# Two quarters to a step in a fused linear-attention and LoRA mixture kernel on one Trainium2 core

## What is computed

```python
def attention(q, k, v):            # EMB_DIM here is the 512 rows, 8 heads of 64
    qh = softmax(qh, axis=3)       # over the rows of a head
    kh = softmax(kh, axis=1)       # over the columns, the kernel's other axis
    kvs = einsum('bnhd,bnhe->bhde', kh, vh)
    return einsum('bnhd,bhde->bnhe', qh, kvs)

def lora_moe(x, router_w, A, B):   # 4 experts, the best 2 are used, rank 16
    logits = flat @ router_w.T
    gates = softmax(top-2 of logits, -inf elsewhere)
    mid = einsum('tf,erf->ter', flat, A)
    all_deltas = einsum('ter,eor->teo', mid, B) * 4
    return einsum('te,teo->to', gates, all_deltas)

x = x + attention(layernorm(x), ctx, ctx)
x = x + lora_moe(layernorm(x), router_w, A, B)
```

## Time and profile before

| | |
|---|---|
| median of three runs | 456.83 us |
| profiled execution | 454.94 us |
| its span | 453.2 us |
| TensorE busy, matmuls / weight loads | 422.5 us (93%) / 382.3 us (84%) |
| VectorE busy | 379.1 us (84%) |
| GpSimd busy | 358.9 us (79%) |
| ScalarE busy | 311.0 us (69%) |
| mean granted TensorE clock | 0.969 of full |
| moved | 137.59 MB, 304 GB/s on average |
| chain that ended last | TensorE 71%, VectorE 10%, GpSimd 6% |

### The profile page before, as it was taken

How to read it: one execution, slowest core, us unless ns; L and a number is a source line. 1 busy time by engine, 2 the same in 40 slices (tenths; PEclk the granted TensorE clock), 3 DMA queues, 4 the chain that set the end, 5 groups by cost and what they waited for, 6 DMA issues and landing times.

```text
span 453.2 us, 16801 instructions
## 1 busy us (share of the span) xinstructions
PE 422.5 (93%) x6888; PEld 382.3 (84%) x6888; DVE 379.1 (84%) x1045; ACT 311.0 (69%) x436; POOL 358.9 (79%) x343
## 2 busy tenths in 40 slices
PE   6558998999999999999999999999999999999975
PEld 6557887898989898998989898998989898999864
DVE  3468777898998989898998989898989989775864
ACT  1265979695968778695958777785959777775310
POOL 0466999999898989898898989898988988994610
PEclk9667999999999999999999999999999999999988
DMA  8995888779999999999999999999999998454247
GB/s 286 420 409 188 307 290 271 248 276 321 364 297 372 339 340 344 307 341 332 351 310 361 331 346 341 307 352 333 357 316 338 310 366 269 173 186 187 95 185 279
DMA packets 38972, 137.59 MB, mean 304 GB/s; under 512 B 4208, under 2 KB 6384, under 8 KB 38768
## 3 DMA queue, kind: packets, MB, share of 16 engines
q1 hardware_dynamic: 38896, 136.52, 86.5%
HBM read 102.95 MB, written 33.55 MB: 301 GB/s over the span
## 4 chain that ended last, share of the span: by engine, by line
PE 71%; DVE 10%; POOL 6%; DMA 4%; issue 3%; SPq 3%; ACT 1%; POOLq 0%; DVEq 0%; ACTq 0%
PE num_ps L407 21%; PE kv_ps L390 14%; PE raw_ps L423 11%; PE delta_ps L471 10%; PE kv_ps L438 6%; PE delta_ps L472 6%; DMA ctx_sb<-in_ctxt_dram 4%; DVE y_sb L709 3%; POOL y_sb L323 3%; POOL ek_sb L311 3%; DVE attnT L700 2%; DVE bn_parts L642 2%; DVE midT L800 1%; PE raw_ps L457 1%; SPq L235 1%
## 5 line engine op out<-in xcount | busy, mean ns | idle before, releaser
L311 POOL TENSOR_TENSOR ek_sb<-ctx_sb,kmax_row 128x512 f32<-128x512 f32 x128 | 167.8, 1313 | 36.5 <-ACT kmax_row L504 36.5
L323 POOL TENSOR_TENSOR y_sb<-attnT,y_sb 128x512 f32<-128x512 f32 x128 | 164.3, 1284 | 31.0 <-DVE attnT L700 31.0
L407 PE MATMUL num_ps<-kv_sb,x_sb 128*128 128x130 f32 x1024 | 141.1, 281 | 9.0 <-DVE attnT L700 6.0
L407 PEld LDWEIGHTS num_ps<-kv_sb,x_sb 128*128 128x128 f32 x1024 | 126.0, 192 | 12.9 <-issue 8.7
L709 DVE TENSOR_TENSOR y_sb<-delta_ps,y_sb 128x512 f32<-128x512 f32 x128 | 87.3, 684 | 23.7 <-PE delta_ps L472 22.8
L625 DVE TENSOR_REDUCE max_n<-ctx_sb 128x32 f32<-128x512 f32 x128 | 86.5, 677 | 10.8 <-DMA ctx_sb<-in_ctxt_dram 10.8
L390 PE MATMUL kv_ps<-ctx_sb,ek_sb 128*64 128x65 f32 x2048 | 92.8, 233 | 0.3 <-ACT ek_sb L526 0.3
L700 DVE TENSOR_TENSOR attnT<-num_ps,rden 128x512 f32<-128x512 f32 x128 | 88.5, 691 | 4.8 <-DVE rden L697 0.4
L390 PEld LDWEIGHTS kv_ps<-ctx_sb,ek_sb 128*64 128x64 f32 x2048 | 74.2, 139 | 17.8 <-issue 5.8
L526 ACT ACTIVATE ek_sb<-ek_sb 128x1024 f32<-128x1024 f32 x64 | 67.1, 1049 | 26.9 <-POOL ek_sb L311 26.9
L423 PE MATMUL raw_ps<-w_sb,y_sb 128*64 128x69 f32 x2048 | 84.5, 223 | 0.0
(11 more groups left out here) (63 smaller groups left out, 398.3 us busy)
## 6 DMA issues: line engine op xcount, KB each, us to landing
ctx_sb<-in_ctxt_dram SPq DMA_DIRECT2D x64, 520.0 KB, 5.3
x_sb<-in_x_dram SPq DMA_DIRECT2D x64, 512.0 KB, 6.1
y_sb<-in_xt_dram SPq DMA_DIRECT2D x64, 512.0 KB, 6.3
out_dram<-y_sb SPq DMA_DIRECT2D x60, 512.0 KB, 6.2
out_dram<-y_sb SPq DMA_DIRECT2D x8, 256.0 KB, 3.6
sq_a<-in_bt_dram SPq DMA_DIRECT2D x1, 1024.0 KB, 15.8
w_sb<-in_wt_dram SPq DMA_DIRECT2D x1, 552.0 KB, 9.6
cst<-in_consts_dram SPq DMA_DIRECT2D x1, 145.0 KB, 2.3
```

What stands on the lines that cost most here:

```text
L311: pool.tensor_tensor(ek_sb[:, t % 2, chunks(g), :].rearrange("p (a b) c -> p a b c", b=2), ctx_sb[:, t % 4, 2 * g:2 * g + 2, 1:P + 1, :].r ...
L323: pool.tensor_tensor(y, attnT[:, g, :], y, ALU.add).then_inc(x1_made, 1)
L407: mm = pe.matmul(num_ps[:, j // 2, at:at + 2 * (DH + 1)], x_sb[:, t % 4, c * P:(c + 1) * P], kv_sb[:, t % 2, :], start=True, stop=True, sk ...
```

## The change

The step becomes two quarters: every engine's loop runs over q in twos, and calls helpers for q and q + 1. FIRST is -10 and LAST is 4 NT + 20. TensorE's calls are put in order by the tile shape they use. The two delta banks become one buffer of two banks, and one `add_delta` takes both. max_ps moves from num_ps to delta_ps. `root1` and `root2` stand between GpSimd's large operations. VectorE's gate and layernorm operations are spread between the large ones, and `normalise` is split into `invert` and `normalise`. The three gate stages stand at offsets 16, 18 and 20, in three consecutive steps. b is loaded after the first ctx, x and y tiles into slot 7 of y_sb, and split in steps 8 to 12. The last stores are four of 512 KB in place of eight of 256 KB.

```diff
-    FIRST = -8
-    LAST = 4 * (NT - 1) + 29
+    FIRST = -10
+    LAST = 4 * NT + 20
...
-        delta_ps = [bank("delta_ps0"), bank("delta_ps1")]
-        max_ps = num_ps[:, 0, 3 * P:4 * P]
+        delta_ps = bank("delta_ps", (P, 2, 512))
+        max_ps = delta_ps[:, 0, 0:P]
...
-            p, i = divmod(q - 21, 8)
+            p, i = divmod(q - 22, 8)
...
             whole(load_ctx, 1)
-            sp.dma_start(w_sb[:], wt).then_inc(w_landed, 16)
             whole(load_x, 1)
             whole(load_ctx, 2)
+            sp.dma_start(w_sb[:], wt).then_inc(w_landed, 16)
             whole(load_y, 0)
-            sp.dma_start(b_rows, bt).then_inc(b_landed, 16)
-            whole(load_y, 1)
             whole(load_x, 2)
             whole(load_ctx, 3)
+            whole(load_y, 1)
+            sp.dma_start(b_rows, bt).then_inc(b_landed, 16)
...
-            for q in range(FIRST, LAST + 1):
-                root1(q)
-                shift(*tile_at(q, -3))
-                root2(q)
-                add_x(*tile_at(q, 5))
+            for q in range(FIRST, LAST + 1, 2):
+                shift(*tile_at(q, -2))
+                add_x(*tile_at(q, 6))
+                root2(pair_in(q, 18))
+                shift(*tile_at(q + 1, -2))
+                root1(tile_in(q, 2))
+                add_x(*tile_at(q + 1, 6))
...
-                after(pe, out_made, 8 * p + i - 1)
+                if i % 2 == 0:
+                    after(pe, out_made, 4 * p + i // 2)
+                    after(pe, kmax_made, min((8 * p + i + 22) // 4 + 2, NT))
...
+            for q in range(FIRST, LAST + 1, 2):
+                turn_max(tile_in(q, -4))
+                numerator(*tile_at(q, 6))
                 delta(*delta_at(q))
-                turn_max(q)
+                delta(*delta_at(q + 1))
+                sum_squares(tile_in(q, 12))
+                turn_mid(pair_in(q, 20))
...
+                spread_kmax(tile_in(q, -4))
+                numerator(*tile_at(q + 1, 6))
+                for k in range(2):
+                    kv(*tile_at(q + k, 0))
+                for k in range(2):
+                    project(*tile_at(q + k, 8))
+                fold_squares(tile_in(q, 10))
...
+            for q in range(FIRST, LAST + 1, 2):
+                T = q // 4
+                if q % 4 == 0:
+                    copy_squares(T - 3)
+                    copy_kv(T - 1)
+                    keys(T, 0)
+                    spread_row(T + 1)
+                    mid_high(pair_in(q, 20))
                     square_x1(T - 2, 0)
+                    queries(T - 1, 0)
                     sum_x(T + 1)
+                else:
                     keys(T, 1)
                     square_x1(T - 2, 1)
+                    gate_exp(pair_in(q, 18))
                     queries(T - 1, 1)
                     square_x(T + 1)
...
             def add_delta(p, i):
-                dve.wait_ge(delta_done, 8 * p + i + 1)
-                y = y_sb[:, pair_slots(p), 2 * i:2 * i + 2, :]
+                dve.wait_ge(delta_done, 8 * p + i + 2)
+                y = y_sb[:, pair_slots(p), 2 * i:2 * i + 4, :]
...
+            for q in range(FIRST, LAST + 1, 2):
+                a, b, c = pair_in(q, 16), pair_in(q, 18), pair_in(q, 20)
+                kv_recip(tile_in(q, 4), 0)
+                if c is not None:
+                    gate_gates(c)
+                kv_recip(tile_in(q, 4), 1)
                 if c is not None:
                     gate_mid(c)
+                max_whole(tile_in(q, -4))
+                invert(*tile_at(q, 6))
+                if b is not None:
+                    gate_rank(b)
+                ln1_bias(tile_in(q, 4))
+                normalise(*tile_at(q, 6))
+                add_delta(*delta_at(q))
+                invert(*tile_at(q + 1, 6))
+                if a is not None:
+                    gate_logits(a)
+                    gate_max(a)
+                if b is not None:
+                    gate_select(b)
+                ln1_mean(tile_in(q, -2))
+                normalise(*tile_at(q + 1, 6))
+                mid_low(c)
+                ln1_aggr(tile_in(q, 0))
                 if a is not None:
                     gate_centre(a)
+                    gate_below(a)
+                    gate_beats(a, 0)
+                    gate_beats(a, 1)
                 if b is not None:
+                    gate_sum(b)
+                    max_part(*tile_at(q, -8))
+                    gate_recip(b)
+                    max_part(*tile_at(q + 1, -8))
+                    gate_scale(b)
+                else:
+                    max_part(*tile_at(q, -8), P // 2)
                 if a is not None:
+                    gate_mask(a)
+                for k in range(2):
+                    bn_part(*tile_at(q + k, -4))
+                ln1_var(tile_in(q, 0))
```

More of the change, by code:

```diff
@@ L791, in gate_mid, with mid_low @@
                         ALU.mult).then_inc(mid_made, 1)
[L793 to L794 removed]
+            def mid_low(p):
                 if p is None:
@@ L801, in mid_low @@
                                   ALU.subtract).then_inc(lo_made, 1)
-            for q in range(FIRST, LAST + 1):
-                early = q < 0
-                if early:
-                    max_whole(q)
-                a, b, c = pair_at(q, 13), pair_at(q, 14), pair_at(q, 15)
-                if b is not None:
-                    gate_beats(b, 0)
+            for q in range(FIRST, LAST + 1, 2):
[4 more added lines that the diff above has]
+                kv_recip(tile_in(q, 4), 1)
@@ L819, in _ @@
-                mid_low(q)
-                bn_part(*tile_at(q, -5))
-                add_delta(*delta_at(q))
-                if a is not None:
-                    gate_logits(a)
-                if b is not None:
-                    gate_rank(b)
-                if not early:
-                    max_whole(q)
-                normalise(*tile_at(q, 5))
-                if a is not None:
-                    gate_below(a)
-                if b is not None:
-                    gate_select(b)
-                    gate_sum(b)
-                    gate_scale(b)
```

196 lines of the change are left out of this document (83 added, 113 removed).

## The result

The changed kernel takes 481.87 us (median of 6 runs, 480.67 to 483.14) against 456.41 us for the kernel before (6 runs): ratio 1.056, 95% interval 1.0539 to 1.0581. Forecast were 467.0 us and a range of 451 to 476. The direction was right, the size lay outside the range. The profiled execution has a span of 479.4 us, 26.2 more than before; forecast were 10.2 more.

The account below looks back on a forecast made before the run. It took TensorE as the bound (24.88 us busy of a 25.24 us pair), VectorE and GpSimd close behind. Start +0.3, steps 22 to 128 +0.2 and end +9.7 sum to +10.2 us: median 467.0 us, range 451 to 476.

Parts of the forecast that it names:

- The start to step 6: Loads of b and second y tile moved back: taken as 5 us, step 6 at 33.3 instead of 38.29.
- The splitting of b: Start, steps 6 to 22: splitting on ScalarE and VectorE now lies here, 1.5 us by estimate.
- The gate's wait in step 18: Start, before step 22: the wait for the gate's exponentials costs 0.9 us.
- the walk: Step-by-step timing of TensorE and VectorE through steps a to d of a pair, giving 25.37 us a pair.
- c's second numerator at 9.74: Steady part, step c: VectorE's product ends at 9.63, the second numerator starts at 9.74 instead of 8.77.
- No price: Items given no cost: max_ps in delta_ps (turn_max's wait), SyncE's list, b's wait before load_y(7).
- TensorE's b ends at 6.42 and is not late yet: Steady part, end of step b: TensorE is on time, so step c's first numerator is at 6.52.
- The gate's wait: Step b, once a pair: gate_select waits for exponentials, VectorE stands still for 1.7 us; 1.0 of the gain goes.
- The end: From step 128: deeper pipeline and last additions in rounds of 3.4 us, 45.6 us against 35.95, +9.7.
- Rival 1: Gate's wait is hidden, TensorE's floor counts: a pair 24.4 or 23.9, 454.2 or 447.6 us; chance 0.18.
- Rival 2: ScalarE becomes late too, waits add 0.6 a pair, 7 us more: 474 us; chance 0.14.
- Rival 3: Changes of shape are not saved, the cost belongs to switches between instruction groups: 482 us; chance 0.06.

Follow-up runs that it names:

- b_early: Changed kernel, but w, b and the second y tile are loaded as in the kernel before, and b is split in steps 0 and 2: 479.22 us.
- start_both: Changed kernel with b loaded and split early (steps 0 and 2) and centre_weights in step 4 instead of 6: 476.58 us.
- root_ahead: Changed kernel, but on GpSimd root2 stands in front of the first add_x of its step instead of behind it: 459.07 us, ratio to before 1.0073.
- max_ahead: Changed kernel, but VectorE takes the context's maxima one step earlier (offset -10 in place of -8): 485.74 us.
- tail_single: Changed kernel, but for the last pair alone the output additions take one bank each: 476.67 us, ratio to before 1.0456.
- sel_exp_late: As sel_late, and on ScalarE the gate's exponentials stand behind queries of the same step: 460.71 us, ratio to before 1.0107.
- sel_late: Changed kernel, but in step b gate_select and the gate's later operations stand behind the second normalise and one merged maximum: 468.19 us, ratio to before 1.0266.
- mid_change: As root_ahead, but the first quarter's kv and project stand between the two numerators, 18 changes of shape a pair instead of 10: 495.95 us.
- centre4: Changed kernel, but centre_weights runs at the end of step 4 in place of step 6: 480.28 us.

## Why the prediction failed where it did

**The start to step 6** (33.3 forecast): 33.1, the right number and in good part luck. The forecast took 5 us for putting the loads back. b_early loads in the old order and has step 6 at 34.6, so the loads are worth 1.4. The rest comes mostly from what a step number stands for. With the numerator at offset 6 in place of 5, step 6 makes the first quarter of tile 0 in the changed kernel and the second in the kernel before, whose first numerator starts at 34.98 (timeline of weight loads, before):

```profile
34.98 1.80 PEld L407 LDWEIGHTS num_ps<-kv_sb,x_sb 128*128 128x128 f32 x8 [3.03 <-ACT kv_sb L556]
```

**Steps 6 to 22: two terms mis-sized.** "The splitting of b ... 1.5 by estimate" and the moved centre_weights, which had no price at all, together cost 6.4 us (start_both), 4.9 more than forecast. The gate's wait in step 18, put at 0.9, costs 1.8 (root_ahead takes 54.6 us between the steps), another 0.9. That is 5.8 of the 6.3. No row that the forecast read showed either block next to a busy GpSimd, but the trace of before had one for b (the last section). The bound of +4 for the start was passed by the measured +6.5 (89.53 against 83.08).

**The steady part: the walk left out a wait and three small pieces of work in step c.** The step that failed is c's second numerator at 9.74. The walk has it wait for the product alone, since "the work between (0.89 + 2 x 0.47 of delta) fills 1.83", and max_ps in delta_ps stands under "No price" for turn_max's wait only. But delta may write into delta_ps only when VectorE has read the maximum there. In the walk itself that is at 8.70, as VectorE is late by the gate's wait; measured, 8.80. Behind it TensorE needs 1.45 us to the second numerator: deltas 0.94 (241.66 to 242.60), and 0.51 (to 243.11) for sum_squares, turn_mid and spread_kmax, which the walk doesn't have at all. So the second numerator comes at 10.37. These 0.63 us are most of the 0.74 that a pair is longer than forecast; the other 0.1 is 0.2 more up to the end of step d, less 0.1 in step a.

"TensorE's b ends at 6.42 and is not late yet" leaves out a second wait, turn_max's for the maxima, which puts c's first numerator at 7.73 instead of 6.52. It is no part of the 0.74: max_ahead takes it away, and c's second numerator and the pair stay where they were. No run takes delta's wait away by itself; that it limits step c is read from the two traces. Where VectorE is on time (root_ahead), c's second numerator still starts 2.41 behind the first instead of 2.25, as sum_squares, turn_mid and spread_kmax stand in between.

From step 22 to 120 took 320.5 us instead of 310.8: twelve pairs at 0.74 are 8.9, and 0.8 come because the stretch begins with a step d, which takes 7.09 where the forecast counted a quarter of 25.37 (6.34). The last pair, without maxima, took 24.6 instead of 23.66, the other 0.9 of the 10.7. The rest of the walk stands: the gap between numerators is 2.2 (232.74 to 234.93), the merged addition 1.22 long, the next operation 1.24 after its start (1.13 estimated), behind a merged maximum 1.13 (232.11 to 233.24; 1.13 estimated), the wait for the product in step d 1.01 (0.96 in the walk).

**The gate's wait** was forecast at its place, cause and size (1.7; 1.87 measured), and root_ahead shows the cause by taking it away. The price was too low. The forecast put the pair without it at 24.4 and got 24.53; with it, 25.37 and got 26.11. So the wait costs 1.58 a pair, not 0.97. The difference is above all delta's wait in step c, which is part of its price.

**The end** (+9.7): +8.8, of which 2.8 go with the gate's wait (root_ahead). The last four additions start at 464.78, 468.17, 471.57 and 474.96, 3.40 apart as forecast, and the clock is at its lower level, 1.2 GHz, as in the earlier trace rows (busy times in a window, then clock, DMA share, GB/s):

```profile
460.00:479.00 19.00, 9.62 (x39) 8.05 (x37) 6.71 (x7) 0.38 (x1) 0.00 (x0) 0.50 0.43 166
```

One of the last rounds, in its timeline:

```profile
469.45 0.58 PE L477 MATMUL delta_ps<-midT,b_hi 128*128 128x256 f32 x1 [1.32 <-DVE y_sb L716]
...
471.57 1.23 DVE L716 TENSOR_TENSOR y_sb<-delta_ps,y_sb 128x1024 f32<-128x1024 f32 x1 [2.17 <-PE delta_ps L478]
```

TensorE waits for VectorE and VectorE for TensorE, in turn. From the last fold (452.74) to the end are 26.7 us; 28 had been named. tail_single gave back 5.2 of the 5.6 that the prediction named for it. By the second half of the rule of the Trainium skill that the prediction weighed (Perfetto Trace Analysis, Optimizing Scalar/DVE Operations), smaller operations may let work finish sooner where the engine isn't saturated but others wait for it. These runs agree, with 5.2 us for the last pair.

**The rivals.** Rival 1 named the right switch point: when the exponentials are there in time, a pair is 24.4. root_ahead and sel_exp_late are that world, at 24.53 and 24.67. It did not hold for the changed kernel. Rival 2, ScalarE late, shows for queries in 2 waits of 1.7 us together, so not as a cause; it became the limit once the gate was moved on VectorE alone (sel_late). Rival 3 is out: the changes were saved, at 0.2 each (mid_change).

## What to carry to other kernels

When a wait is forecast on an in-order engine, list everything queued behind it up to the next step and, for each piece, who needs it and in which order: here the delayed multiplication was priced, but not the reading of a maximum behind it, which held the next step's delta matmuls because the maximum shares their buffer. A large wait in a list of waits need not cost anything: turn_max's 1.2 us a pair stood in front of another that ended as late without it. Ask of a small chain over several engines where its links would fall into time that an engine waits anyway; three short operations (L346 to L351) moved ahead of a waiting addition gave 22.8 us of 482. And in mid_change the place of a shared buffer's second use in a step mattered more than the changes of tile shape around it. Last, before a time at a step number is compared between two kernels, see that the number stands for the same piece of work in both.

## What the hardware showed that was not expected

Beside GpSimd's work, VectorE's subtractions take longer, and GpSimd's work with them. The same two subtractions of b (128x512, both inputs in SBUF) take 1.29 us in steps 0 and 2 of b_early, with no GpSimd instruction in between, and 3.46 in step 10 of the changed kernel beside two of GpSimd, of which one is itself longer (1.72, mean 1.31). First b_early, then the changed kernel (timelines):

```profile
26.86 1.29 DVE L864 TENSOR_TENSOR b_lo<-y_sb,b_hi 128x512 fp32r<-128x512 f32 x2 [6.66 <-ACT b_hi L618]
```

```profile
54.64 1.28 POOL L333 TENSOR_TENSOR y_sb<-attnT,y_sb 128x512 f32<-128x512 f32 x1
54.70 3.46 DVE L864 TENSOR_TENSOR b_lo<-y_sb,b_hi 128x512 fp32r<-128x512 f32 x2
55.89 1.72 POOL L321 TENSOR_TENSOR ek_sb<-ctx_sb,kmax_row 128x512 f32<-128x512 f32 x1
...
59.23 0.13 PEld L383 LDWEIGHTS kv_ps<-cst,kmax 128*128 128x128 f32 x1 [2.25 <-DVE kmax L638]
```

The last row is what it cost TensorE. centre_weights likewise takes 2.39 in step 6 and 1.29 in step 4 (centre4). VectorE's maxima and bn_stats, with one input, and its operations that read PSUM keep their length beside GpSimd (0.68, 0.69 and 1.22 in the timeline of the pair above).

The trace of the kernel before had the same, in its splitting of b (timeline of VectorE): the first subtraction has no GpSimd instruction beside it, the second one of 1.30 from 26.92.

```profile
25.76 0.69 DVE L843 TENSOR_TENSOR b_lo<-sq_a,b_hi 128x512 fp32r<-128x512 f32 x1 [6.10 <-ACT b_hi L614]
...
27.15 1.62 DVE L843 TENSOR_TENSOR b_lo<-sq_a,b_hi 128x512 fp32r<-128x512 f32 x1
```

The Trainium skill (SBUF — State Buffer, Who interferes with whom) says that a VectorE instruction with two inputs in SBUF contends with a GpSimd instruction that reads SBUF, and that the later of the two waits for all of the earlier one. The changed kernel's trace agrees on the whole: the four instructions (two of each engine) take 3.52 us (54.64 to 58.16), nearer to one after the other (1.28 + 1.31 + 1.29 = 3.88) than to side by side (2.59).

Earlier in the start, after TensorE's wait of 3.48 for kmax, up to 43.90, its granted clock was 0.60 from 42 to 50 us, a mean of its two levels, and the eight weight loads of a numerator took 1.80 instead of 0.97. From step 6 to 22 the mean is 0.93, as in start_both, and 0.99 in the kernel before; what that difference costs was not told apart.
